# Another order of VectorE's and GpSimd's work in a pair of the cross attention

## The chip, the cores and the metric

The kernel runs on one core of a Trainium2 chip. Its metric is the device time of one execution in microseconds (us). Before the change the median of three runs is 623.79 us, and the runs lie between 623.78 and 624.98 us.

## The reference

One decoder layer on x of shape 4 x 1024 x 256 (32 tiles of 128 rows), with a context of 4 x 77 x 256, all in float32:

```python
x = _layernorm(x + attn(x))            # single head, layer-normed q and k, sigmoid(scores/16 - log S), layerscale
x = _layernorm(x + xattn(ctx, ctx, x)) # 16 heads of 16, softmax over 77 keys, dense
x = _layernorm(x + ffn(x))             # token shift, sigmoid gate, relu squared
```

The change touches the middle line: `logits = q k' / 4` per head, `softmax(logits)`, the product with the values, `dense`, the sum with x, and the second layer norm.

## The kernel before, in words

Every engine has its own instruction queue, written out by hand, and works through it in order; semaphores join the queues. There are three stages. The first is the self attention with the first norm. The second is the cross attention, and the third the feed-forward part. The change is in the second stage alone.

The second stage is a loop over s, one pair of tiles (2s and 2s+1, 256 rows) each, for s = 0 to 15, with three more rounds (16 to 18) that drain it and in which the third stage begins. It is pipelined by hand: in round s the queues hold the logits, maxima and exponentials of pair s, the transposition of the softmax weights of tiles 2s-3 and 2s-2, the product with the values of pair s-2, the dense product and residual of pair s-3, and the second norm of pairs s-3 and s-4. In the same round the query of pair s+2 is made from the normed x.

For one tile t the chain is as follows. TensorE makes the logits (`cross_scores`, L1230) in two halves. VectorE takes the maxima of each half (`maxima`, L846). ScalarE makes the exponentials (`exponentials`, L389). GpSimd adds the halves of a row (`fold_weights`, L607), VectorE sums them (`sums`, L852) and inverts (`reciprocals`, L859), and GpSimd multiplies (`normalise`, L612). TensorE turns the weights in three blocks (`weights_t`, L1246); VectorE copies the first two out (`weights_body`, L866), and ScalarE the third (`weights_tail`, L319). The three blocks of all tiles share two PSUM banks in turn, so a block can be turned only when the block two before it has been copied out. The products with the values (`mixed`, L1263) go to ScalarE and VectorE as a high and a low part (`mixed_hi`, `mixed_lo`, L728), and then to `dense`.

The query of pair s+2 needs a transposition (`x1`), its high part on ScalarE (`x1_hi`) and its low part on VectorE (`x1_lo`, L728); TensorE's `query` is the last item of its round.

The second norm of a pair: VectorE adds the residual (`crossed`, L879) and makes the statistics (`stats2`, L884 and L889). GpSimd makes the deviation and the bias (`deviation2`, L621 to L626). ScalarE norms the first tile (`norm2`, L319) and VectorE the second (`norm2`, a tensor_scalar from SBUF to SBUF, L894). `norm1` (L808) is an instruction of the same kind and shape on VectorE; four of them stand in round 2.

VectorE's queue in a round, in order: `maxima(2s,0)`, `weights_body(2s-3,0)`, `crossed(s-3)`, `maxima(2s,1)`, `weights_body(2s-3,1)`, `sums` and `reciprocals(2s-1)`, `x1_lo(s+2)`, `maxima(2s+1,0)`, `stats2(s-3)`, `weights_body(2s-2,0)`, `mixed_lo(s-2)`, `maxima(2s+1,1)`, `weights_body(2s-2,1)`, `sums` and `reciprocals(2s)`, `norm2(s-4)`.

GpSimd's queue in a round: `fold_weights(2s-1)`, `residual2(s)` (L599), `normalise(2s-1)`, `deviation2(s-3)`, `fold_weights(2s)`, `normalise(2s)`.

ScalarE's queue in a round: `exponentials(2s,0)`, `weights_tail(2s-3)`, `exponentials(2s,1)`, `x1_hi(s+2)`, `norm2(s-4)`, `exponentials(2s+1,0)`, `mixed_hi(s-2)`, `exponentials(2s+1,1)`, `weights_tail(2s-2)`, `query(s+2)`.

TensorE's queue in a round: `cross_scores(2s,0)`, `dense(s-3)`, `weights_t(2s-3,0)`, `cross_scores(2s,1)`, `weights_t(2s-3,1)` and `(2s-3,2)`, `x1(s+2)`, `cross_scores(2s+1,0)`, `weights_t(2s-2,0)`, `mixed(s-2)`, `cross_scores(2s+1,1)`, `weights_t(2s-2,1)` and `(2s-2,2)`, `query(s+2)`.

Of the kernel before, what the change touches and what calls it, by code (L numbers as in the profile page):

```python
# [22 lines left out]
NJ = NT // 2  # L23
# [48 lines left out]
def decoder_layer(nc, io):  # L72
    ctx = ExitStack()
    with ctx:
# [162 lines left out]
        def weights(t):  # L237
            return p_sb[:, t % NP].rearrange("p (h k) -> p h k", k=SP)
# [13 lines left out]
        with nc.Block() as block:  # L252
# [271 lines left out]
            def _(pool):  # L524
# [39 lines left out]
                def deviation1(g):  # L564
                    w.wait_ge(*ln1s_dve.at(g))
                    if g:
                        w.wait_ge(*ln1b_dve.at(g - 1))
                    pool.tensor_tensor(rsl[:], mvl[:, :, 1], eps4, ALU.add).then_inc(ln1s_pool.sem, 1)
                    w.wait_ge(*ln1s_pool.at(g, 1))
                    pool.tensor_tensor(rsl[:], rsl[:], half4, ALU.pow).then_inc(ln1s_pool.sem, 1)  # L570
# [25 lines left out]
                def residual2(i):  # L596
                    w.wait_ge(*tx_pe.at(i))
                    x2 = xs[:, 2 * i:2 * i + 2, :]
                    pool.tensor_tensor(x2, x2, each_tile(bxd[:], 2), ALU.add).then_inc(xr_pool.sem, 1)  # L599

                def fold_weights(t):
                    w.wait_ge(*ex_act.at(4 * t + 3))
                    w.wait_ge(*pads_pool.at(0))
                    if t:
                        w.wait_ge(*sum_dve.at(t - 1))
                    p = weights(t)
                    pool.tensor_tensor(fold[:].rearrange("p (h k) -> p h k", k=FO), p[:, :, 0:FO],  # L607
                                       p[:, :, FO:2 * FO], ALU.add).then_inc(fo_pool.sem, 1)

                def normalise(t):  # L610
                    w.wait_ge(*rc_dve.at(t))
                    pool.tensor_tensor(weights(t), weights(t), rc[:, t % 2].rearrange("p (h o) -> p h o", o=1)  # L612
                                       .to_broadcast([P, H, SP]), ALU.mult).then_inc(pn_pool.sem, 1)

                def deviation2(i):
                    w.wait_ge(*xds_dve.at(i))
                    if i >= 2:
                        w.wait_ge(*ln2_act.at(i - 2))
                        w.wait_ge(*ln2_dve.at(i - 2))
                    r, nb = rs2[:, i % 2], nb2[:, i % 2]  # L620
                    pool.tensor_tensor(r, mv2[:, i % 2, :, 1], eps4[:, 0:2], ALU.add).then_inc(xds_pool.sem, 1)  # L621
                    pool.tensor_tensor(nb, mv2[:, i % 2, :, 0], minus4[:, 0:2], ALU.mult).then_inc(xds_pool.sem, 1)
                    w.wait_ge(*xds_pool.at(i, 1))
                    pool.tensor_tensor(r, r, half4[:, 0:2], ALU.pow).then_inc(xds_pool.sem, 1)
                    w.wait_ge(*xds_pool.at(i, 3))
                    pool.tensor_tensor(nb, nb, r, ALU.mult).then_inc(xds_pool.sem, 1)  # L626
# [64 lines left out]
                for s in range(NJ + 3):  # L691
                    if 1 <= s <= NJ:
                        fold_weights(2 * s - 1)
                        if s < NJ:
                            residual2(s)
                        normalise(2 * s - 1)
                    if s == 1:
                        deviation1(NG - 1)
                    if 0 <= s - 3 < NJ:
                        deviation2(s - 3)  # L700
                    if s < NJ:
                        fold_weights(2 * s)
                        normalise(2 * s)
                    if s == 0:
                        tail_rows()
                    for i in (2 * (s - NJ) - 1, 2 * (s - NJ)):
                        if i >= 0:
                            halo(i)
                            if i >= 3:
                                residual3(i - 3)  # L710
                            if i >= 4:
                                deviation3(i - 4)
                                norm3(i - 4)
# [10 lines left out]
            def _(dve):  # L724
                w = Once(dve)

                def low_part(hi, lo, whole):
                    return dve.tensor_tensor(lo, whole, f(hi), ALU.subtract)  # L728
# [65 lines left out]
                def stats1(g):  # L794
                    for t in range(4):
                        w.wait_ge(*ln1a_dve.at(g, t // 2 + 1))
                        dve.bn_stats(stl[:, t], xs[:, 4 * g + t]).then_inc(ln1s_dve.sem, 1)
                    if g:
                        w.wait_ge(*ln1s_pool.at(g - 1))
                    for t in range(4):  # L800
                        w.wait_ge(*ln1s_dve.at(g, 1 + t))
                        dve.bn_aggr(mvl[:, t], stl[:, t]).then_inc(ln1s_dve.sem, 1)
# [34 lines left out]
                def x1_lo(i):  # L837
                    w.wait_ge(*tx_act.at(i))
                    low_part(*hi_lo(x1T, i % 2), x_bank).then_inc(tx_dve.sem, 1)
# [15 lines left out]
                def reciprocals(t):  # L855
                    w.wait_ge(*sum_dve.at(t))
                    if t >= 2:
                        w.wait_ge(*pn_pool.at(t - 2))
                    dve.reciprocal(rc[:, t % 2], sm[:, t % 2]).then_inc(rc_dve.sem, 1)  # L859
# [9 lines left out]
                def mixed_lo(i):  # L869
                    w.wait_ge(*pv_act.at(i))  # L870
                    if i >= 2:
                        w.wait_ge(*xd_pe.at(i - 2))
                    low_part(*hi_lo(oT, i % 2), pv_bank).then_inc(pv_dve.sem, 1)
# [7 lines left out]
                def stats2(i):  # L881
                    w.wait_ge(*xda_dve.at(i))
                    for t in range(2):
                        dve.bn_stats(st2[:, i % 2, t], xs[:, 2 * i + t]).then_inc(xds_dve.sem, 1)  # L884
                    if i >= 2:
                        w.wait_ge(*xds_pool.at(i - 2))
                    for t in range(2):
                        w.wait_ge(*xds_dve.at(i, 1 + t))
                        dve.bn_aggr(mv2[:, i % 2, t], st2[:, i % 2, t]).then_inc(xds_dve.sem, 1)  # L889
# [134 lines left out]
                for s in range(NJ + 3):  # L1024
                    if 0 < s < NJ:
                        maxima(2 * s, 0)
                    if 0 <= 2 * s - 3 < NT:
                        weights_body(2 * s - 3, 0)
                    if 0 <= s - 3 < NJ:
                        crossed(s - 3)  # L1030
                    if 0 < s < NJ:
                        maxima(2 * s, 1)
                    if 0 <= 2 * s - 3 < NT:
                        weights_body(2 * s - 3, 1)
                    if 1 <= s <= NJ:
                        sums(2 * s - 1)
                        reciprocals(2 * s - 1)
                    if s + 2 < NJ:
                        x1_lo(s + 2)
                    if s < NJ:  # L1040
                        maxima(2 * s + 1, 0)
                    if s == 2:
                        norm1(NG - 1)
                    if 0 <= s - 3 < NJ:
                        stats2(s - 3)
                    if 0 <= 2 * s - 2 < NT:
                        weights_body(2 * s - 2, 0)
                    if 0 <= s - 2 < NJ:
                        mixed_lo(s - 2)
                    if s < NJ:  # L1050
                        maxima(2 * s + 1, 1)
                    if s == 0:
                        stats1(NG - 1)
                    if 0 <= 2 * s - 2 < NT:
                        weights_body(2 * s - 2, 1)
                    if s < NJ:
                        sums(2 * s)
                        reciprocals(2 * s)
                    if 0 <= s - 4 < NJ:
                        norm2(s - 4)  # L1060
                    for i in (2 * (s - NJ) - 1, 2 * (s - NJ)):
                        if i >= 0:
                            if i >= 1:
                                mix_lo(i - 1)
                            if i >= 3:
                                stats3(i - 3)
                            mixes(i)
                            if i >= 2:
                                gated(i - 2)
                            if i >= 1:  # L1070
                                key_squares_lo(i - 1)
# [387 lines left out]
```

## Time and profile before

| what | value |
|---|---|
| median of three runs | 623.79 us |
| the profiled execution's own time | 621.29 us |
| its span (first to last instruction) | 619.2 us |
| mean granted TensorE clock | 0.982 |
| PE, DVE, ACT, POOL busy over the span | 551.2, 453.1, 366.4, 344.9 us |
| chain that ended last: PE, DVE, ACT, POOL | 58%, 15%, 12%, 6% |

The second stage runs from about 301 us to about 506 us of the span. PE is TensorE, DVE is VectorE, ACT is ScalarE and POOL is GpSimd. A busy time is the time in which an engine worked on instructions, and successive instructions of DVE and ACT overlap by some 0.08 to 0.13 us in the trace, so the cost of one in a queue is the distance between two starts. The chain is followed back from the last instruction of the program to what released each step.

### The profile page before, as it was taken

Reading aid. Unit: us, or ns where it says so; the run is one execution under the profiler, and the core shown is the slowest. Engines: PE = TensorE matmul, PEld = TensorE weight load, DVE = VectorE, ACT = ScalarE, POOL = GpSimd, SP = SyncE. Lnnn points to the kernel's source line nnn. Section 1 sums busy time; section 2 is a strip of 40 time slices with the busy share of each in tenths; the row PEclk is TensorE's granted clock in tenths of the full one; section 3 lists DMA queues with packets and bytes.
Section 4 is the critical chain, followed back from the end, with each engine's and each line's share of the span. In section 5 each row is a group of like instructions: output and inputs, shape, how many; then the busy total and the mean of one; then the engine's idle time right before and its main releaser. Section 6 shows DMA issues by size and latency. Waiting matters only on the chain.

```text
span 619.2 us, 11109 instructions
## 1 busy us (share of the span) xinstructions
PE 551.2 (89%) x3952; PEld 455.2 (74%) x3952; DVE 453.1 (73%) x1050; ACT 366.4 (59%) x984; POOL 344.9 (56%) x377
## 2 busy tenths in 40 slices
PE   3879999999999999999868998999899968798884
PEld 2769989898989899888645665666566557788883
DVE  3976566777766676765467788888888976898885
ACT  1245444344444444433676788788878847788882
POOL 3545253433525351415177687788778960588885
PEclk9999999999999999999987999999999998999998
DMA  5221001010130002100000000000000000011112
GB/s 174 68 69 48 23 0 52 19 52 18 51 104 1 1 25 77 52 2 0 2 0 2 1 1 2 2 2 1 2 2 1 2 2 1 17 36 52 52 48 72
DMA packets 18351, 17.53 MB, mean 28 GB/s; under 512 B 1836, under 2 KB 18297, under 8 KB 18297
## 3 DMA queue, kind: packets, MB, share of 16 engines
q1 hardware_dynamic: 18024, 16.57, 8.4%
q8 instruction: 31, 0.51, 0.3%
q10 hardware_dynamic: 272, 0.26, 0.1%
q14 instruction: 24, 0.19, 0.1%
HBM read 12.63 MB, written 4.19 MB: 27 GB/s over the span
## 4 chain that ended last, share of the span: by engine, by line
PE 58%; DVE 15%; ACT 12%; POOL 6%; issue 5%; DMA 1%; SPq 1%; POOLq 0%; DVEq 0%; ACTq 0%
PE ring L215 29%; PE big L215 17%; PE ring L1246 4%; ACT p_sb L389 4%; PE big L1230 3%; POOL p_sb L612 2%; PE ring L1139 2%; DVE neg_mx L846 2%; POOL fold L607 2%; DVE pT L866 2%; DVE kkT_lo L728 1%; DVE st L884 1%; ACT kr L440 1%; ACT kkT_hi L450 1%; ACT pT L319 1%
## 5 line engine op out<-in xcount | busy, mean ns | idle before, releaser
L389 ACT ACTIVATE p_sb<-big,neg_mx 128x77 f32<-128x77 f32 x384 | 89.8, 344 | 34.9 <-DVE neg_mx L846 34.9
L728 DVE TENSOR_TENSOR aT_lo<-a_sb,aT_hi 128x512 fp32r<-128x512 f32 x64 | 45.6, 712 | 79.0 <-ACT aT_hi L319 79.0
L612 POOL TENSOR_TENSOR p_sb<-p_sb,rc 128x1248 f32<-128x1248 f32 x32 | 73.1, 2283 | 31.8 <-DVE rc L859 31.8
L1246 PE MATMUL ring<-ident,p_sb 128*128 128x128 f32 (+1 forms) x384 | 58.7, 283 | 21.8 <-DVE pT L866 20.4
L215 PE MATMUL big<-vv_hi,aT_hi 128*128 128x256 f32 x256 | 72.7, 284 | 3.4 <-DVE xs L792 3.4
L352 ACT ACTIVATE a_sb<-ring,nlogs 128x512 f32<-128x512 f32 x64 | 43.5, 680 | 53.6 <-PE ring L215 53.5
L1246 PEld LDWEIGHTS ring<-ident,p_sb 128*128 128x128 f32 (+1 forms) x384 | 39.6, 130 | 46.0 <-DVE pT L866 23.6
L215 PE MATMUL big<-vv_hi,aT_lo 128*128 128x256 f32 x256 | 72.4, 283 | 0.0
L215 PE MATMUL big<-vv_lo,aT_hi 128*128 128x256 f32 x256 | 72.4, 283 | 0.0
L1230 PE MATMUL big<-kb,xq 64*128 64x308 f32 x192 | 51.5, 481 | 4.7 <-ACT p_sb L389 4.0
L215 PEld LDWEIGHTS big<-vv_hi,aT_hi 128*128 128x128 f32 x256 | 48.8, 191 | 8.1 <-issue 5.8
L215 PE MATMUL ring<-qkT_hi 128*128 128x512 f32 x128 | 51.7, 404 | 0.0
L607 POOL TENSOR_TENSOR fold<-p_sb 128x624 f32<-128x624 f32 x32 | 48.8, 1524 | 4.7 <-ACT p_sb L389 4.7
L215 PEld LDWEIGHTS big<-vv_lo,aT_hi 128*128 128x128 f32 x256 | 48.8, 191 | 2.2
L215 PE MATMUL ring<-qkT_lo,qkT_hi 128*128 128x512 f32 x128 | 50.2, 392 | 0.0
L215 PE MATMUL ring<-qkT_hi,qkT_lo 128*128 128x512 f32 x128 | 49.9, 390 | 0.0
L546 POOL TENSOR_TENSOR rs<-mv,consts 128x2 f32<-128x2 f32 x32 | 12.5, 391 | 65.9 <-DVE mv L760 65.9
L215 PEld LDWEIGHTS big<-vv_hi,aT_lo 128*128 128x128 f32 x256 | 48.8, 191 | 0.0
L866 DVE COPY pT<-ring 128x512 f32<-128x512 f32 x64 | 43.6, 681 | 5.0 <-PE ring L1246 5.0
L846 DVE TENSOR_REDUCE neg_mx<-big 128x4 f32<-128x308 f32 x96 | 42.2, 468 | 2.3 <-PE ring L1230 2.1
L556 POOL TENSOR_TENSOR vv_lo<-v_sb,vv_hi 128x512 fp32r<-128x512 f32 x16 | 21.1, 1316 | 40.5 <-ACT vv_hi L319 40.5
L319 ACT ACTIVATE xT_hi<-xraw 128x512 fp32r<-128x512 f32 x16 | 10.1, 631 | 55.7 <-PE big L215 50.0
(160 smaller groups left out, 1757.1 us busy)
## 6 DMA issues: line engine op xcount, KB each, us to landing
xraw<-in_xT SPq DMA_DIRECT2D x16, 256.0 KB, 2.6
xs<-in_x SPq DMA_DIRECT2D x8, 512.0 KB, 3.9
out_y<-y SPq DMA_DIRECT2D x16, 256.0 KB, 2.1
cT<-in_cT SPq DMA_DIRECT2D x1, 308.0 KB
wraw<-in_wqT ACTq DMA_DIRECT2D x1, 256.0 KB, 3.9
wraw<-in_wkT SPq DMA_DIRECT2D x1, 256.0 KB, 4.3
wv_raw<-in_wv SPq DMA_DIRECT2D x1, 256.0 KB, 5.8
wo_ls<-in_woT SPq DMA_DIRECT2D x1, 256.0 KB, 5.7
```

What stands on the lines that cost most here:

```text
L215: mm = pe.matmul(out, s_, m_, start=first and k == 0 and q == 0, stop=last and k == n - 1 and q == 2, skip_group_check=not check)
L319: return act.activation(out, in_, ACT.Identity, **kw)
L352: act.activation(a_sb[:, i % NAR], st_bank[i % 2], ACT.Sigmoid, bias=nlogs[:, 0:1], scale=1.0 / 16).then_inc(st_act.sem, 1)
L389: ex = act.activation(weights(t)[:, HG * g + h, 0:SC], logits[g][:, h * SC:(h + 1) * SC], ACT.Exp, bias=neg_mx[:, t % 2, HG * g + h:HG * g ...
L556: pool.tensor_tensor(lo, tiles(v_sb[:, i % 2]), f(hi), ALU.subtract).then_inc(v_pool.sem, 1)
L607: pool.tensor_tensor(fold[:].rearrange("p (h k) -> p h k", k=FO), p[:, :, 0:FO], p[:, :, FO:2 * FO], ALU.add).then_inc(fo_pool.sem, 1)
L612: pool.tensor_tensor(weights(t), weights(t), rc[:, t % 2].rearrange("p (h o) -> p h o", o=1) .to_broadcast([P, H, SP]), ALU.mult).then_inc ...
L728: return dve.tensor_tensor(lo, whole, f(hi), ALU.subtract)
L846: dve.tensor_reduce(neg_mx[:, t % 2, HG * g:HG * (g + 1)], logits[g][:, 0:LW].rearrange("p (h k) -> p h k", k=SC), AX, ALU.min)\
L866: dve.tensor_copy(pT[:, t // 2 % 2, c, :, (t % 2) * P:(t % 2 + 1) * P], tiles(tp_bank[(3 * t + c) % 2], NH)).then_inc(tp_dve.sem, 1)
L1230: mm = pe.matmul(logits[2 * e + r][:, 0:LW], xq[half, i % 2, e * D + u * P:e * D + (u + 1) * P], kb[half, b, e], start=True, stop=True)
L1246: mm = pe.transpose(tp_bank[n % 2][0:rows, g * P:(g + 1) * P], p_sb[:, t % NP, c0:c0 + rows], ident[:])
```

## The change

VectorE's queue in a round gets another order in its second half, and `deviation2` on GpSimd goes behind `normalise(2s)`. No instruction is added or removed.

```diff
@@ GpSimd
                         deviation1(NG - 1)
-                    if 0 <= s - 3 < NJ:
-                        deviation2(s - 3)
                     if s < NJ:
                         fold_weights(2 * s)
                         normalise(2 * s)
+                    if 0 <= s - 3 < NJ:
+                        deviation2(s - 3)
@@ VectorE
                         sums(2 * s - 1)
                         reciprocals(2 * s - 1)
-                    if s + 2 < NJ:
-                        x1_lo(s + 2)
                     if s < NJ:
                         maxima(2 * s + 1, 0)
                     if s == 2:
                         norm1(NG - 1)
-                    if 0 <= s - 3 < NJ:
-                        stats2(s - 3)
                     if 0 <= 2 * s - 2 < NT:
                         weights_body(2 * s - 2, 0)
-                    if 0 <= s - 2 < NJ:
-                        mixed_lo(s - 2)
+                    if s + 2 < NJ:
+                        x1_lo(s + 2)
                     if s < NJ:
                         maxima(2 * s + 1, 1)
                     if s == 0:
                         stats1(NG - 1)
+                    if 0 <= s - 2 < NJ:
+                        mixed_lo(s - 2)
                     if 0 <= 2 * s - 2 < NT:
                         weights_body(2 * s - 2, 1)
                     if s < NJ:
                         sums(2 * s)
                         reciprocals(2 * s)
+                    if 0 <= s - 3 < NJ:
+                        stats2(s - 3)
                     if 0 <= s - 4 < NJ:
                         norm2(s - 4)
```

## Rows read from the trace of the kernel before

**Rows 1.** Busy time by engine over one round (stretch, length, then busy, count).
```profile
389.10:401.46 12.36, 11.45 (x102) 7.97 (x102) 10.62 (x25) 10.28 (x41) 9.95 (x10) 1.00 0.01 2
```

**Rows 2.** Chain that ended last: one step in two rounds (start, length).
```profile
399.40 0.62 PE ring L1246 x4
...
411.76 0.62 PE ring L1246 x4
```

**Rows 3.** Timeline of DVE in one round (start, length, idle before and releaser).
```profile
390.50 0.32 DVE L894 TENSOR_SCALAR xs<-xs,mv,rs 128x256 f32<-128x256 f32 x1
...
394.47 0.80 DVE L852 TENSOR_REDUCE sm<-fold 128x16 f32<-128x624 f32 x1
395.31 0.25 DVE L859 RECIPROCAL rc<-sm 128x16 f32<-128x16 f32 x1
396.42 0.69 DVE L728 TENSOR_TENSOR x1T_lo<-ring,x1T_hi 128x512 fp32r<-128x512 f32 x1 [0.85 <-ACT x1T_hi L319]
397.02 0.47 DVE L846 TENSOR_REDUCE neg_mx<-big 128x4 f32<-128x308 f32 x1
...
397.80 0.74 DVE L884 BATCH_NORM_STATS2 st<-xs 128x6 f32<-128x256 f32 x2
...
398.67 0.67 DVE L866 COPY pT<-ring 128x512 f32<-128x512 f32 x1
399.89 0.69 DVE L728 TENSOR_TENSOR oT_lo<-ring,oT_hi 128x512 fp32r<-128x512 f32 x1 [0.54 <-ACT oT_hi L319]
```

**Rows 4.** Timeline of ACT in the same round.
```profile
393.62 0.59 ACT L319 ACTIVATE pT<-ring 56x512 f32<-56x512 f32 x1 [0.29 <-PE ring L1246]
394.11 1.79 ACT L389 ACTIVATE p_sb<-big,neg_mx 128x77 f32<-128x77 f32 x8
395.78 0.61 ACT L319 ACTIVATE x1T_hi<-ring 128x512 fp32r<-128x512 f32 x1
396.25 0.62 ACT L319 ACTIVATE xs<-xs,nb,rs 128x256 f32<-128x256 f32 x1
...
399.20 0.65 ACT L319 ACTIVATE oT_hi<-ring 128x512 fp32r<-128x512 f32 x1
```

**Rows 5.** All instructions of L808 (count, then shortest, median, longest in ns).
```profile
L808 DVE TENSOR_SCALAR xs<-xs,mvl,rsl x32: 398/408/1595, 93.8 to 334.0; 128x256 f32<-128x256 f32 x32
```

**Rows 6.** Timelines of DVE and POOL in round 2.
```profile
331.25 0.97 DVE L808 TENSOR_SCALAR xs<-xs,mvl,rsl 128x256 f32<-128x256 f32 x1
...
329.80 2.28 POOL L612 TENSOR_TENSOR p_sb<-p_sb,rc 128x1248 f32<-128x1248 f32 x1
332.03 1.56 POOL L607 TENSOR_TENSOR fold<-p_sb 128x624 f32<-128x624 f32 x1
```

**Rows 7.** Timelines of DVE and PE in round 14.
```profile
480.41 0.68 DVE L866 COPY pT<-ring 128x512 f32<-128x512 f32 x1
...
483.67 0.79 PE L1230 MATMUL big<-kb,xq 64*128 64x308 f32 x4
```

**Rows 8.** Timeline of POOL, normalise of tiles 26, 30 and 31.
```profile
477.21 2.29 POOL L612 TENSOR_TENSOR p_sb<-p_sb,rc 128x1248 f32<-128x1248 f32 x1 [1.41 <-DVE rc L859]
...
499.56 2.29 POOL L612 TENSOR_TENSOR p_sb<-p_sb,rc 128x1248 f32<-128x1248 f32 x1 [1.20 <-DVE rc L859]
...
504.53 2.28 POOL L612 TENSOR_TENSOR p_sb<-p_sb,rc 128x1248 f32<-128x1248 f32 x1 [1.20 <-DVE rc L859]
```

**Rows 9.** Timeline of DVE in rounds 16 and 17.
```profile
504.37 0.69 DVE L884 BATCH_NORM_STATS2 st<-xs 128x6 f32<-128x256 f32 x2
...
505.19 0.67 DVE L866 COPY pT<-ring 128x512 f32<-128x512 f32 x1
...
515.03 0.69 DVE L728 TENSOR_TENSOR oT_lo<-ring,oT_hi 128x512 fp32r<-128x512 f32 x1 [1.96 <-ACT oT_hi L319]
```

**Rows 10.** Timeline of POOL, first instructions of deviation2 and the fold behind it.
```profile
484.42 0.20 POOL L621 TENSOR_TENSOR rs<-mv,consts 128x2 f32<-128x2 f32 x1
...
485.65 1.52 POOL L607 TENSOR_TENSOR fold<-p_sb 128x624 f32<-128x624 f32 x1
```

## The prediction

> **What bounds the kernel now.** I read the busy time by engine over one round first. In the middle of the second stage TensorE works 11.45 us of a round and no other engine over 10.62 us [rows 1]. The chain that ended last repeats itself every 411.76 - 399.40 = 12.36 us [rows 2], so a round costs 0.91 us more than TensorE's work. The chain passes through tail copy and exponentials on ScalarE, x1_hi, then on VectorE x1_lo, maxima(2s+1,0), stats2 and the copy of a turned block, and only then back to TensorE. In VectorE's timeline the reader sees why: after the reciprocal (ends 395.56) it sits idle 0.85 us for x1_lo, then come maxima and statistics, and the copy that frees TensorE's bank ends only at 399.34 [rows 3]; the transposition of the third block starts at 399.40 [rows 2]. It idles 0.54 us more for mixed_lo [rows 3].
>
> **What the change takes away.** After the reciprocal stand now maxima(2s+1,0), whose logits are ready, and the copy. The copy ends 0.77 + 0.68 = 1.45 us after the start of the maxima, about 397.0 and not 399.34. TensorE's 0.91 us go, and the next bound would be TensorE's own 11.45 us, if nothing else grows. GpSimd loses nothing by its edit at first sight: deviation2 (1.23 us, from 484.42 to the fold at 485.65 [rows 10]) goes behind normalise(2s), and fold(2s) comes earlier.
>
> **What it adds.** No instruction is new, so the question is what each now stands beside. The pair's end is reciprocals(2s), stats2, norm2. GpSimd starts normalise(2s) 0.08 us after the reciprocal ends (at 504.53, the reciprocal ends 504.45, which is 0.08 us behind the start of the statistics [rows 8, 9]) and works on it 2.28 us. Statistics do not mind: beside exactly such a normalise they took 505.19 - 504.37 = 0.82 us, against 398.67 - 397.80 = 0.87 us with GpSimd idle [rows 3, 8, 9]. But norm2 is a tensor_scalar from SBUF to SBUF. Before, it started at 390.50, directly behind the reciprocal and ahead of normalise, and took 0.32 us [rows 3]. Its sister L808 shows what happens behind the start of a GpSimd instruction: median 408 ns, but 966 ns for the one issued at 331.25 while normalise ran (329.80 to 332.08); it ended at 332.22, 0.14 us after GpSimd's instruction. The one behind it met the fold (332.03 to 333.59) and is the longest of all, 1595 ns [rows 5, 6]. So such an instruction waits until the running GpSimd instruction is over, and ends 0.14 us later. The Trainium skill, page "SBUF — State Buffer", section on SBUF's two separate sides, gives the reason: VectorE in a two-port mode and GpSimd share one port pair, which whoever starts first holds for its whole instruction. By that rule, the trace agrees. This rule speaks against the change.
>
> In the new order norm2 is issued 0.74 us after the reciprocal's end (0.82 - 0.08), while normalise runs until 0.08 + 2.28 = 2.36. It ends at 2.50, not at 1.06: a stall of 1.44 us per round, from round 4, the first with a norm2.
>
> **The round, walked with the stall.** Zero is the end of reciprocals(2s-2). Costs in a queue are distances between starts (length less 0.08 us of overlap): maxima of one half pair 0.77, copy 0.60, each of x1_lo, mixed_lo and crossed 0.60 (all 512 wide with one operand in PSUM), sums 0.84, reciprocal 0.25 [rows 3].
> VectorE: maxima(2s,0) at 2.42, copy 3.19, crossed 3.79, maxima(2s,1) 4.39, copy (2s-3,1) 5.16, sums 5.76, reciprocal 6.60 to 6.85, maxima(2s+1,0) 6.77, copy 7.54, x1_lo 8.14, free at 8.74. GpSimd is in time: normalise 2.36, deviation2 3.59, fold(2s-1) 5.1, against sums at 5.76.
> TensorE: the copy at 5.16 frees block (2s-2,0). In round 14 it was 483.67 + 0.79 - 480.41 = 4.05 us from that copy's start to the end of the logits (2s+1,1) [rows 7]; so maxima(2s+1,1) starts at 5.16 + 4.07 = 9.23, VectorE is free again at 10.00.
> ScalarE: its first exponentials start 0.51 us behind the maxima (0.47 for the first bank, 0.04 to react), at 2.93; a half tile is 395.78 - 394.11 = 1.67 us. Then tail copy 0.49, exponentials 1.67, x1_hi 0.47, its own norm2 0.49 (0.62 less the overlap), exponentials 1.67: mixed_hi starts at 9.39 and mixed_lo 0.69 us later (399.89 - 399.20), at 10.08 [rows 3, 4]. The tail copy does not wait longer: TensorE turns its block 0.62 us behind the copy of 3.19 (ends 3.87), ready about 4.55; ScalarE comes at 4.60.
> VectorE again: copy 10.68, sums 11.28, reciprocal 12.12 to 12.37. **The new round takes about 12.37 us**, against 12.36 us. The loop that closes is ScalarE's row of work plus VectorE's end of the pair; TensorE, with 0.9 us idle again, is not it.
>
> **The ends of the stage.** All in time against before; minus is earlier.
> - Rounds 0 to 3: no norm2, so no stall; there TensorE's 0.9 us are gained once (round 3), and some tenths in rounds 0 to 2, which hang on GpSimd and on norm1 (pinned by GpSimd's two instructions of rows 6). I take -1.1 at reciprocals(25).
> - Within a round the second normalise now comes sooner after the first: 12.37 - 6.85 = 5.5 us. Before it was 7.4: mixed_lo at 399.89, then 0.60 + 0.77 + 0.60 + 0.84 + 0.25 to 402.95, from 395.56 [rows 3]. That is a shift of -1.9, so normalise(26), at 477.21 before, comes at -3.0.
> - Rounds 14 and 15 have no x1 and no query. Before, GpSimd bound them: 499.56 - 477.21 = 22.35 us for two [rows 8]. Now the stall stays: maxima(2s+1,1) ends at 10.00, mixed_lo follows at once, 12.3 us a round, 24.6 for two. +2.25, sum -0.75.
> - normalise(30) to normalise(31) was 4.97 us [rows 8]; deviation2 now stands between, +1.23, sum +0.5.
> - Round 16: the statistics no longer stand ahead of the copy of 505.19 [rows 9], -0.82, sum -0.3.
> - Round 17: the statistics stood in the idle 1.96 us ahead of mixed_lo (515.03) [rows 9]; now they stand behind it and ahead of the third stage's low parts, +0.87, sum +0.6.
> With nine rounds at +0.01 the sum is +0.6 to +0.7 us. The profiled execution, 621.29 us of which 619.2 are its span, would become 621.9. It lies 2.5 us under the median of 623.79; I add the difference to the median: **624.4 us**.
>
> The unknown costs, from both sides. Of a round: 0.1 us less, if ScalarE's exponentials react faster (its maxima and starts lie 0.47 to 0.51 us apart), or 0.15 us more, if the tail copy waits (its margin is 0.05 us); eleven rounds make -1.1 and +1.7. Of the moved mixed_lo and x1_lo: nothing to 0.1 us, since both have later readers. Rounds 0 to 3: -2 to 0; TensorE's clock there is part of that, because in round 2 it idles some 3 us in both orders. Main case: 622.4 to 626.8.
>
> **The rivals.**
> - *The stall does not come* (norm2 isn't held, or the statistics push it to where it is harmless). For it: the median of L808's 32 is 408 ns. Against: those had no long GpSimd instruction beside them; here normalise always starts first. Then VectorE's round is 12.37 - 1.44 = 10.9, GpSimd's loop, by rounds 14 and 15 that it bound, 22.35 / 2 = 11.2 [rows 8], and TensorE's 11.45 binds: -0.91 for nine rounds, -8.2, with -3.0 at normalise(26) as above, nothing in rounds 14 and 15, +1.2 for deviation2 behind them, and -0.82 and +0.87 at the end: about -10, 613.8 us.
> - *Half of it*: ScalarE or TensorE arrives so that only 0.5 us of the stall counts in the loop. A round of 11.9 us, -0.45 for nine rounds, -4.1, with the ends as in the main case: 620.3 us.
> - *Slower: the stall makes ScalarE's tail copy late.* The place is round s's first tail copy: TensorE turns its block only behind VectorE's copy of 3.19, which the stall moves. From the point at which that block is ready later than 4.60, each tenth is a tenth per round. With 0.3 us (TensorE still busy with dense when the copy is done) it is 12.7 a round and eleven times 0.3: +3.3, 627.7 us. For it: a margin of 0.05 us. Against: TensorE has 0.9 us to spare.
> - *Nothing moves*: as before within 0.3 us, 623.8. It can't be told from the main case.
>
> **How the numbers follow.** A measurement of this kernel can tell about 0.2% from no change, 1.25 us: faster is below 622.5, slower above 625.0. Main case with its twin 0.62, of which 0.04 below 622.5 and 0.19 above 625.0; no stall 0.11; half 0.10; tail copy late 0.17. Faster 0.25, same 0.39, slower 0.36. The range for 8 in 10 is 619.5 to 628.2; it leaves out the case without a stall. The main case's own is 622.4 to 626.8.
>
> **What would show it.** Right: L894 with a mean near 1.76 us instead of 0.32, each ending about 0.14 us behind a normalise; the round at 12.3 to 12.5 us; TensorE's waits for the third block's bank gone from (2s-2,2) but its work still near 11.45 of the round, with waits spread over (2s-3,2) and (2s-2,0); rounds 14 and 15 near 12.3 us and not 11.2; normalise(2s) directly behind its reciprocal with deviation2 behind it without a wait. Wrong: L894 still at 0.32 us, a round of 11.4 to 11.6 us, TensorE without idle time in the middle of the stage; or a tail copy that waits over 0.3 us for TensorE.

## The result: 0.67% slower, and the profile after

The changed kernel takes 627.92 us, the median of 18 runs between 625.16 and 630.78, against 623.75 us for the kernel before (18 runs, 620.89 to 625.33). The ratio is 1.0067 with a 95% interval of 1.0047 to 1.0087: 4.2 us slower in the medians. The profiled execution took 626.28 us with a span of 624.5 us, 5.3 us more than the span before. A second profile of the same kernel (below, `r_after_again`) has a span of 624.3 us and the same pattern. Where span times are compared below, they are single profiled executions.

The busy time over one round of the changed kernel, between two starts of normalise(2s) (as in [rows 1]: behind the length, the busy time and number of instructions of TensorE, of its weight loads, of VectorE, ScalarE and GpSimd):

```profile
398.98:411.34 12.36, 11.50 (x101) 7.97 (x102) 11.79 (x25) 10.01 (x41) 9.96 (x9) 1.00 0.01 2
```

The round is 12.36 us long, as before [rows 1, 2]. VectorE is now busy 11.79 us of it and not 10.62. Its own timeline shows with what, and GpSimd's beside it shows why:

```profile
399.64 1.77 DVE L894 TENSOR_SCALAR xs<-xs,mv,rs 128x256 f32<-128x256 f32 x1
```
```profile
398.98 2.28 POOL L612 TENSOR_TENSOR p_sb<-p_sb,rc 128x1248 f32<-128x1248 f32 x1 [1.76 <-DVE rc L859]
401.22 0.24 POOL L621 TENSOR_TENSOR rs<-mv,consts 128x2 f32<-128x2 f32 x1
```

normalise(2s) ends at 398.98 + 2.28 = 401.26, and norm2 at 399.64 + 1.77 = 401.41, 0.15 us later. Before, it took 0.32 us [rows 3]. It is so in all twelve rounds with both, 4 to 15; the other four, in the drain, meet no long GpSimd instruction and take 0.38 to 0.40 us. The row of all sixteen (shortest, median, longest in ns):

```profile
L894 DVE TENSOR_SCALAR xs<-xs,mv,rs x16: 381/1767/1769, 362.6 to 546.7; 128x256 f32<-128x256 f32 x16
```

The chain that ended last, from the stall through the rest of that round (start, length; x2 is two instructions). The reader sees that it runs along VectorE and crosses to TensorE only for block (2s-2,0), the product with the values and one half of the logits:

```profile
399.64 1.38 DVE xs L894
401.33 0.85 DVE neg_mx L846 x2
402.18 0.60 DVE pT L866
402.78 0.60 DVE xs L879
403.38 0.77 DVE neg_mx L846 x2
404.15 0.61 DVE pT L866
404.89 0.63 PE ring L1246 x4
405.52 1.86 PE ring L1263 x32
407.38 0.74 PE big L1230 x4
408.15 0.86 DVE neg_mx L846 x2
409.01 0.64 DVE oT_lo L728
```

Where the rounds end up in time is read from normalise of tiles 26, 28, 30 and 31 in GpSimd's timeline, to be laid beside [rows 8]:

```profile
473.11 2.28 POOL L612 TENSOR_TENSOR p_sb<-p_sb,rc 128x1248 f32<-128x1248 f32 x1 [1.76 <-DVE rc L859]
...
485.41 2.28 POOL L612 TENSOR_TENSOR p_sb<-p_sb,rc 128x1248 f32<-128x1248 f32 x1 [1.72 <-DVE rc L859]
...
497.71 2.28 POOL L612 TENSOR_TENSOR p_sb<-p_sb,rc 128x1248 f32<-128x1248 f32 x1 [1.72 <-DVE rc L859]
503.94 2.27 POOL L612 TENSOR_TENSOR p_sb<-p_sb,rc 128x1248 f32<-128x1248 f32 x1 [1.20 <-DVE rc L859]
```

Up to normalise(31) the changed kernel is not slower at all, but 504.53 - 503.94 = 0.6 us ahead. All of the loss comes behind it. Rounds 16 and 17, the drain, lose 5.5 us, and the rest of the third stage 0.4 us: -0.6 + 5.5 + 0.4 = 5.3 us of span. In the drain VectorE's timeline runs:

```profile
506.90 0.69 DVE L728 TENSOR_TENSOR oT_lo<-ring,oT_hi 128x512 fp32r<-128x512 f32 x1 [2.50 <-ACT oT_hi L319]
...
510.65 1.67 DVE L916 SCALAR_TENSOR_TENSOR big<-ring,mu,carry 128x256 f32<-128x256 f32 x4 [1.28 <-POOL carry L633]
...
519.07 0.69 DVE L728 TENSOR_TENSOR oT_lo<-ring,oT_hi 128x512 fp32r<-128x512 f32 x1 [4.97 <-ACT oT_hi L319]
519.68 0.74 DVE L884 BATCH_NORM_STATS2 st<-xs 128x6 f32<-128x256 f32 x2
...
520.56 0.38 DVE L894 TENSOR_SCALAR xs<-xs,mv,rs 128x256 f32<-128x256 f32 x1
520.85 1.28 DVE L728 TENSOR_TENSOR xmT_lo<-big,xmT_hi 128x512 fp32r<-128x512 f32 x2
```

The same two instructions of the third stage, its first mixes (L916) and its first low part (L728 of xmT), in the kernel before:

```profile
508.75 1.67 DVE L916 SCALAR_TENSOR_TENSOR big<-ring,mu,carry 128x256 f32<-128x256 f32 x4 [1.35 <-ACT carry L319]
...
515.96 1.28 DVE L728 TENSOR_TENSOR xmT_lo<-big,xmT_hi 128x512 fp32r<-128x512 f32 x2
```

The third stage's first low part starts 520.85 - 503.94 = 16.9 us behind normalise(31). Before it was 515.96 - 504.53 = 11.4 us, so 5.5 us are lost here. This distance is called the drain's length below. TensorE's timeline in the drain says what is slow:

```profile
500.79 0.62 PE L1246 MATMUL ring<-ident,p_sb 128*56 128x128 f32 x4 [2.15 <-DVE pT L866]
...
503.02 3.17 PE L1263 MATMUL ring<-pT,vb 128*32 128x256 f32 x32
...
512.96 1.06 PE L1246 MATMUL ring<-ident,p_sb 128*56 128x128 f32 x4 [2.76 <-DVE pT L866]
514.75 3.64 PE L1263 MATMUL ring<-pT,vb 128*32 128x256 f32 x32 [0.73 <-DVE pT L866]
```

The products with the values of pairs 14 and 15 take 3.17 and 3.64 us; before, both took 1.93:

```profile
502.49 1.93 PE L1263 MATMUL ring<-pT,vb 128*32 128x256 f32 x32
...
512.41 1.93 PE L1263 MATMUL ring<-pT,vb 128*32 128x256 f32 x32 [0.73 <-ACT pT L319]
```

TensorE had idled 2.15 us for the copy behind norm2(11), which stalls at the end of round 15, and 2.76 us in round 17; in the kernel before these two waits were 0.28 and 1.80 us. In the rows by stretch the third number from the end is the granted clock, a mean between 1.00 (2.4 GHz) and 0.50 (1.2 GHz). TensorE was at the lower level for a part of each stretch below; before, it was 1.00 all the way from 500 to 516 us:

```profile
500.00:504.00 4.00, 2.54 (x20) 1.51 (x24) 3.13 (x7) 1.08 (x2) 2.72 (x6) 0.77 0.00 0
504.00:508.00 4.00, 4.00 (x43) 2.43 (x36) 1.50 (x3) 1.34 (x3) 2.22 (x1) 0.80 0.01 4
...
512.00:516.00 4.00, 2.31 (x17) 1.19 (x21) 2.10 (x4) 1.84 (x4) 0.00 (x0) 0.55 0.00 0
516.00:520.00 4.00, 3.40 (x28) 1.61 (x20) 0.93 (x2) 1.16 (x3) 0.00 (x0) 0.59 0.00 0
```

### The profile page after: what moved, and what is told of

It reads as the page before. It is cut to its first block, busy times and chain, and to the rows that moved or that the text cites. A ratio compares the mean times of both kernels' runs of the same rounds, so it can differ in the third digit from the quotient of the medians.

```text
span 624.5 us, 11109 instructions
## 1 busy us (share of the span) xinstructions
PE 553.6 (89%) x3952; PEld 454.9 (73%) x3952; DVE 468.2 (75%) x1050; ACT 363.2 (58%) x984; POOL 345.1 (55%) x377
## 4 chain that ended last, share of the span: by engine, by line
PE 55%; DVE 26%; ACT 7%; issue 6%; POOL 4%; DMA 1%; SPq 1%; POOLq 0%; DVEq 0%; ACTq 0%
PE ring L215 24%; PE big L215 17%; PE ring L1263 5%; DVE neg_mx L846 4%; DVE pT L866 3%; DVE xs L894 3%; PE ring L1246 2%; PE big L1230 2%; PE ring L1139 2%; DVE sm L852 2%; DVE st L884 1%; DVE kkT_lo L728 1%; DVE oT_lo L728 1%; DVE xs L879 1%; ACT kr L440 1%
## 5 line engine op out<-in xcount | busy, mean ns | idle before, releaser
L728 DVE TENSOR_TENSOR aT_lo<-a_sb,aT_hi 128x512 fp32r<-128x512 f32 x64 | 45.6, 712 | 78.9 <-ACT aT_hi L319 78.9
L1230 PE MATMUL big<-kb,xq 64*128 64x308 f32 x192 | 50.1, 471 | 4.7 <-ACT p_sb L389 4.0
```

The costliest lines, as they stand in the source:

```text
L1230: mm = pe.matmul(logits[2 * e + r][:, 0:LW], xq[half, i % 2, e * D + u * P:e * D + (u + 1) * P], kb[half, b, e], start=True, stop=True)
```

## The experiments

Theory A: the stall of norm2 eats what the new order of maxima and copies gains. Theory C: the drain loses time by the place of stats2 in it, and, C2, by TensorE's clock. Theory D: the drain is late through the last stall, that of round 15. The rivals are those of each run's own expectation. Each ratio is to the kernel before in runs on the same chip; that kernel's median differs between chips (620.6 to 623.4 us), so ratios are compared and not times.

### Theory A

**norm2 ahead of the statistics** (`e1_norm2_first`), changed kernel with

```diff
                         reciprocals(2 * s)
-                    if 0 <= s - 3 < NJ:
-                        stats2(s - 3)
                     if 0 <= s - 4 < NJ:
                         norm2(s - 4)
+                    if 0 <= s - 3 < NJ:
+                        stats2(s - 3)
```

> The changed kernel with one swap: norm2 on VectorE stands directly behind the second reciprocals, ahead of stats2, so that it is issued before normalise(2s) starts. Theory A (the stall of 1.44 us a round, VectorE's tensor_scalar held by GpSimd's running instruction, is what eats the gain): L894 falls from 1.77 to 0.32 us, the round from 12.36 to 11.4 to 11.6 us, TensorE has no idle time in the middle of the stage; rounds 14 and 15 take about 11.2 us; the time is 9 to 12 us under the changed kernel's 627.9, near 617. Rival B (the stall is beside the limit, ScalarE's or TensorE's loop holds the round at 12.36 us anyway): L894 short again, the round still 12.2 us or more, the time within 2 us of 627.9.

Measured: 612.08 us, ratio 0.9868 (0.9842 to 0.9894). L894's instructions, and one round, between two starts of a normalise:

```profile
L894 DVE TENSOR_SCALAR xs<-xs,mv,rs x16: 320/322/855, 361.1 to 532.2; 128x256 f32<-128x256 f32 x16
```
```profile
401.31:412.57 11.26, 11.26 (x107) 8.01 (x103) 10.42 (x25) 10.15 (x40) 9.88 (x10) 1.00 0.00 1
```

The swap of two neighbours is worth 2% against the changed kernel (0.9868 against 1.0067). TensorE has no idle time in the round any more; the round is 11.26 us, even below the 11.4 expected. The longest of L894, 855 ns, is norm2(12) in the drain: there it comes behind the start of normalise(31) and ends 492.89 + 0.85 = 493.74, again 0.14 us after it (491.32 + 2.28 = 493.60). The drain is 505.45 - 491.32 = 14.1 us long, so this version still loses 2.7 us there; the product of pair 15 took 3.04 us.

**The stall alone** (`e4_stall_alone`), kernel before with

```diff
                         maxima(2 * s, 0)
+                    if 5 <= s < NJ:
+                        norm2(s - 5)
...
-                    if 0 <= s - 4 < NJ:
+                    if 0 <= s - 4 < NJ and s >= NJ - 1:
                         norm2(s - 4)
```

> The kernel before, with one instruction moved in rounds 5 to 14: norm2 on VectorE goes behind maxima(2s,0) of the next round, so that it is issued 0.8 us after normalise started. Nothing else is changed. Theory A: L894 takes 1.5 to 1.8 us instead of 0.32 in those rounds, VectorE's copy of the first turned block and maxima(2s,1) come 1.1 us later, ScalarE's chain 0.6 to 1.1 us later, the round is 13.0 to 13.4 us and the time 6 to 10 us over the kernel before. Rival (an instruction of this kind isn't held by GpSimd's; L808's long ones have another cause): L894 stays at 0.32 us and the time within 0.5 us of the kernel before.

Measured: 631.75 us, ratio 1.0164 (1.0128 to 1.0200), 11 us slower for one small instruction moved by one place. All of L894, then the same tile's normalise in two successive rounds:

```profile
L894 DVE TENSOR_SCALAR xs<-xs,mv,rs x16: 320/1876/1879, 366.1 to 552.8; 128x256 f32<-128x256 f32 x16
```
```profile
371.57 2.28 POOL L612 TENSOR_TENSOR p_sb<-p_sb,rc 128x1248 f32<-128x1248 f32 x1 [1.04 <-DVE rc L859]
...
384.69 2.28 POOL L612 TENSOR_TENSOR p_sb<-p_sb,rc 128x1248 f32<-128x1248 f32 x1 [1.04 <-DVE rc L859]
```

A round is 13.12 us, 0.76 more than before. In the old order about half of the 1.55 us of stall reaches the loop. The 11 us are more than the 6 to 10 expected. In the profile TensorE's clock fell as well: the products of pairs 13 and 15 took 3.00 and 3.39 us instead of 1.93, so not all of the 11 us is the stall.

**The second tile's norm on ScalarE** (`e11_norm2_on_scalar`), changed kernel with ScalarE's norm2 doing both tiles and VectorE's taken out

```diff
+                    copy(xs[:, 2 * i + 1], xs[:, 2 * i + 1], bias=nb2[:, i % 2, 1:2], scale=rs2[:, i % 2, 1:2])\
+                        .then_inc(ln2_dve.sem, 1)
...
-                    if 0 <= s - 4 < NJ:
-                        norm2(s - 4)
...
-                norm2(NJ - 1)
```

> The changed kernel with the second tile's norm2 moved from VectorE to ScalarE; VectorE keeps its new order otherwise, stats2 at the pair's end. Theory A (port shared by VectorE's tensor_scalar and GpSimd's instruction): no instruction is held any more, since ScalarE's of the same shape took 0.62 us beside GpSimd's work; ScalarE's row of work grows by 0.5 us a round; VectorE's shrinks by 1.7; a round of 11.3 to 11.6 us and 8 to 10 us under the changed kernel in its rounds. Rival B (whatever norms the second tile waits there, for the deviation or for xs, not for the port): ScalarE shows an instruction of over 1 us or an idle time ahead of it, and the round stays at 12 us or more.

Measured: 614.26 us, ratio 0.9889 (0.9863 to 0.9916). ScalarE's two norms take 1.11 us together, with no wait ahead and none inside; normalise of tile 2s comes every 408.98 - 397.55 = 11.43 us:

```profile
403.31 1.11 ACT L319 ACTIVATE xs<-xs,nb,rs 128x256 f32<-128x256 f32 x2
```
```profile
397.55 2.28 POOL L614 TENSOR_TENSOR p_sb<-p_sb,rc 128x1248 f32<-128x1248 f32 x1 [1.32 <-DVE rc L861]
...
403.73 2.27 POOL L614 TENSOR_TENSOR p_sb<-p_sb,rc 128x1248 f32<-128x1248 f32 x1
...
408.98 2.28 POOL L614 TENSOR_TENSOR p_sb<-p_sb,rc 128x1248 f32<-128x1248 f32 x1 [1.48 <-DVE rc L861]
```

ScalarE norms the same rows with the same deviations, partly beside a normalise (403.73 to 406.00), and nothing is held or waits for data. Rival B, that the norm waits for its data, falls.

This run also says something of the drain. It has the changed order of stats2 there and no stall, and TensorE's clock stayed at 1.00 from 480 to 504 us, also behind a wait of 2.49 us. Its timelines of GpSimd, TensorE and VectorE:

```profile
494.21 2.28 POOL L614 TENSOR_TENSOR p_sb<-p_sb,rc 128x1248 f32<-128x1248 f32 x1 [1.20 <-DVE rc L861]
...
500.56 0.62 PE L1245 MATMUL ring<-ident,p_sb 128*56 128x128 f32 x4 [2.49 <-DVE pT L868]
501.91 1.93 PE L1262 MATMUL ring<-pT,vb 128*32 128x256 f32 x32 [0.73 <-ACT pT L319]
...
506.01 1.25 DVE L730 TENSOR_TENSOR xmT_lo<-big,xmT_hi 128x512 fp32r<-128x512 f32 x2
```

The drain is 506.01 - 494.21 = 11.8 us long, against 11.4 before and 16.9 in the changed kernel.

**Maxima and copy alone** (`e5_maxima_copy_only`), kernel before with

```diff
-                    if s + 2 < NJ:
-                        x1_lo(s + 2)
                     if s < NJ:
                         maxima(2 * s + 1, 0)
                     ...
-                    if 0 <= s - 3 < NJ:
-                        stats2(s - 3)
                     if 0 <= 2 * s - 2 < NT:
                         weights_body(2 * s - 2, 0)
+                    if s + 2 < NJ:
+                        x1_lo(s + 2)
+                    if 0 <= s - 3 < NJ:
+                        stats2(s - 3)
```

> The kernel before with one part of the change alone: maxima(2s+1,0) and the copy of the turned block stand ahead of x1_lo and stats2; norm2, mixed_lo and GpSimd's order as before. Theory A: no stall (L894 at 0.32 us), TensorE's 0.91 us of a round are gained at least in part. deviation2 stands ahead of fold(2s) and waits for the statistics, about as long as before, so GpSimd's loop decides: a round of 11.5 to 12.0 us and 4 to 9 us under the kernel before. Rival (the gain needs all of the new order, mixed_lo behind the maxima above all, since ScalarE's loop holds the round): 12.2 us or more a round, within 2 us of the kernel before.

Measured: 613.12 us, ratio 0.9852 (0.9816 to 0.9888), 10.3 us under the kernel before (623.38 on its chip), more than the 4 to 9 expected. One round:

```profile
398.37:410.08 11.71, 11.43 (x103) 7.97 (x101) 10.53 (x25) 10.12 (x40) 9.92 (x9) 1.00 0.01 2
```

These moves alone bring all but about half a per cent of the most that any version here reached (0.9804).

### Theory C: the drain

**Statistics at the old place in the drain** (`e3_old_drain`), changed kernel with

```diff
+                    if NJ <= s and s - 3 < NJ:
+                        stats2(s - 3)
                     if 0 <= 2 * s - 2 < NT:
                         weights_body(2 * s - 2, 0)
...
-                    if 0 <= s - 3 < NJ:
+                    if 3 <= s < NJ:
                         stats2(s - 3)
```

> The changed kernel, but in rounds 16 to 18 stats2 is at its old place; rounds 0 to 15 as changed, the stall with them. Theory C (statistics' place in the drain costs some 2 us ahead of the first mixes and 0.9 us ahead of the third stage's low parts): 2 to 4 us under the changed kernel, 624 to 626, the first mixes about 5 us behind normalise(31) instead of 6.7. Rival D (the drain is late because norm2 of round 15 holds VectorE 1.4 us, TensorE idles 2.15 us and its clock is granted at half): under 1 us gained, the products with the values of pairs 14 and 15 still at 3.2 and 3.7 us.

Measured: 623.30 us, ratio 1.0028 (1.0011 to 1.0045), so the old order in the drain gives back 0.4 to 0.5% of the kernel's time. From normalise(31) to the first low part it is 516.47 - 505.04 = 11.4 us, as before, with norm2(11) still stalled (1.76 us). TensorE's two products are at full speed, though the first comes behind the same wait of 2.15 us as in the changed kernel:

```profile
501.89 0.62 PE L1248 MATMUL ring<-ident,p_sb 128*56 128x128 f32 x4 [2.15 <-DVE pT L866]
...
503.74 1.93 PE L1265 MATMUL ring<-pT,vb 128*32 128x256 f32 x32
...
512.92 1.93 PE L1265 MATMUL ring<-pT,vb 128*32 128x256 f32 x32 [0.73 <-ACT pT L319]
```

The clock fell in this profile too, only earlier, in round 15, in which nothing differs from the changed kernel. The row of that stretch has a granted clock of 0.72; the product of pair 13 took 3.08 us, and normalise(30) came 498.82 - 491.75 = 7.1 us behind normalise(29) instead of 5.5:

```profile
490.00:496.00 6.00, 5.62 (x48) 2.77 (x45) 3.26 (x8) 4.50 (x19) 4.91 (x3) 0.72 0.00 0
```

So the gain is measured, but this run can't tell how much of it is the order and how much a clock that fell at a cheaper place.

**The last stall taken out** (`e6_last_stall_out`), changed kernel with norm2 ahead of stats2 for `s >= NJ - 1` only.

```diff
+                    if s >= NJ - 1 and 0 <= s - 4 < NJ:
+                        norm2(s - 4)
                     if 0 <= s - 3 < NJ:
                         stats2(s - 3)
-                    if 0 <= s - 4 < NJ:
+                    if 0 <= s - 4 < NJ and s < NJ - 1:
                         norm2(s - 4)
```

> The changed kernel, but from round 15 on norm2 on VectorE stands ahead of stats2, so that the stall of round 15 (which delays the copy that TensorE waits 2.15 us for) is gone and the ten before it stay. Theory D (the drain is late through that stall): TensorE's idle time there falls to about 0.8 us, its clock stays at full speed behind it, and the time falls 2 to 4 us below the changed kernel. Rival C (order of the statistics alone): only the 1.4 us of the stall or less, since in the drain GpSimd's chain of folds and multiplications has slack for it.

Measured: 626.67 us, ratio 1.0060 (1.0037 to 1.0082), against 1.0081 (1.0056 to 1.0105) for the changed kernel on the same chip. The intervals overlap: inconclusive. In its profile TensorE's idle time ahead of the third block is 0.74 us and the product of pair 14 takes 1.93 us, as theory D has it, but that of pair 15 takes 3.26 us, and the clock had also fallen in round 15 (the product of pair 13 took 2.35 us). The drain is 522.11 - 507.91 = 14.2 us long.

**Filler for TensorE** (`e7_filler`), changed kernel with 14 transpositions of the identity, read by nobody, in each round from 16 on

```diff
                         weights_t(2 * s - 3, 1)
+                        if s >= NJ:
+                            filler(14)
                         weights_t(2 * s - 3, 2)
```

> The changed kernel with work added that computes nothing: 14 transpositions of the identity into a bank nobody reads, ahead of the third turned block in each of rounds 16 to 18, where TensorE waits 2.15 and 2.76 us. Theory C2 (the drain costs its 5.9 us mostly because TensorE's granted clock falls to half behind those idle times): the products with the values of pairs 14 and 15 take 1.9 us again instead of 3.2 and 3.7, and the time falls 2 to 3 us below the changed kernel though it does more. Rival: the clock isn't what costs; the same time or up to 1 us more.

Measured: 625.07 us (12 runs, 622.42 to 628.62), ratio 1.0029 (1.0005 to 1.0053). TensorE's two products:

```profile
503.05 1.93 PE L1268 MATMUL ring<-pT,vb 128*32 128x256 f32 x32
...
513.08 3.58 PE L1268 MATMUL ring<-pT,vb 128*32 128x256 f32 x32 [0.73 <-ACT pT L319]
```

More work, less time: the first product is at full speed again, the second isn't. The interval ends just below that of the changed kernel on the same chip (1.0056 to 1.0105); the medians lie 3.3 us apart, against 2 to 3 us expected. So the clock is a real part of the loss, and filler ahead of the wait does not hold it everywhere.

**The changed kernel once more** (`r_after_again`).

> The changed kernel again, unaltered, for a comparison on the same chip as the next ones: 4 us over the kernel before (ratio 1.0067), runs spread over several us. If the drain's loss is TensorE's clock (theory C2), the profile shows in each such execution a stretch at half clock between about 500 and 525 us, at a place that may differ from that of the first profile.

Measured: 628.41 us, ratio 1.0081 (1.0056 to 1.0105). In its profile the two products take 3.54 and 3.64 us.

### Versions that beat both

**norm2 ahead, and the old drain** (`e2_norm2_first_old_drain`): the edits of `e1_norm2_first` and `e3_old_drain` together.

> As the one with norm2 ahead of stats2, and in rounds 16 to 18 (in which the stage drains) VectorE's stats2 is at its old place ahead of the copies and mixed_lo. Theory A with theory C (the changed order costs up to 5 us in the drain, through the statistics on the way to the third stage and TensorE's lower clock behind its longer idle times): round 11.4 to 11.6 us and the drain, from normalise(31) to the first product of the third stage, back near 12.2 us from 17.7; 10 us under the kernel before, about 613 to 615. Rival D (the drain's cost came with the stall of norm2 in round 15, not with the order of the statistics): the same time as the kernel with norm2 ahead alone, within 1 us.

Measured: 610.93 us, ratio 0.9841 (0.9823 to 0.9858). The difference from 0.9868 isn't resolved. The expectation counts the drain up to the first product of the third stage, 516.70 - 504.53 = 12.2 us before; here that is 505.49 - 491.77 = 13.7 us. Up to the first low part it is 504.75 - 491.77 = 13.0 us, against 11.4. The product of pair 15 took 3.47 us, behind a wait of 1.80 us, as long as the one in the kernel before, behind which it took 1.93.

**The same with filler** (`e8_best_filler`).

> The kernel with norm2 ahead and the old drain, plus the 14 transpositions of the identity in each of rounds 16 to 18. Theory C2 (TensorE's clock at half for two stretches near 500 and 507 us is what still costs in the drain): the product with the values of pair 15 at 1.9 us instead of 3.5 and 1 to 2 us gained over its twin without filler, ratio about 0.981. Rival: the clock falls elsewhere instead, no gain (0.984).

Measured: 610.36 us, ratio 0.9818 (0.9791 to 0.9844); the drain 504.15 - 492.73 = 11.4 us, and both products took 1.93 us. The gain over its twin is within the intervals.

**norm2 ahead, and stats2 behind the first copy in the drain** (`e9_norm2_first_drain2`).

```diff
                         x1_lo(s + 2)
+                    if NJ <= s and s - 3 < NJ:
+                        stats2(s - 3)
...
-                    if 0 <= s - 3 < NJ:
-                        stats2(s - 3)
                     if 0 <= s - 4 < NJ:
                         norm2(s - 4)
+                    if 3 <= s < NJ:
+                        stats2(s - 3)
```

> The best of both: the changed order in rounds 0 to 15 with norm2 on VectorE ahead of stats2, and in rounds 16 to 18 stats2 directly behind the first copy and ahead of mixed_lo (where the kernel with maxima and copy alone has it, with the shortest drain seen, 11.0 us from normalise(31) to the third stage's first low part). Theory: rounds of 11.27 us as with norm2 ahead, drain 11 to 13 us: 1 to 2 us below the kernel with the old drain's 0.984 of the kernel before, a ratio of 0.982. Rival: the drain depends on where TensorE's clock falls and not on this place; ratio 0.984 to 0.987.

Measured: 609.20 us, ratio 0.9804 (0.9779 to 0.9830), the lowest ratio of all, 12.7 us under the kernel before on its chip (621.92); from 0.9818 and 0.9841 it isn't resolved. Its drain takes 501.92 - 490.90 = 11.0 us and both products 1.93 us:

```profile
488.19 1.93 PE L1265 MATMUL ring<-pT,vb 128*32 128x256 f32 x32
...
498.37 1.93 PE L1265 MATMUL ring<-pT,vb 128*32 128x256 f32 x32 [0.73 <-ACT pT L319]
```

## Why the prediction was right where it was, and where it was not

The forecast was 624.4 us in a range of 619.5 to 628.2; the time is 627.92, inside it but near its upper end. The likeliest class was no change; it is a slowdown, for which the chance was 0.36. That the range holds is in part luck. The main case's own range ends at 626.8, below the measured time; what reached up to 628.2 was the room for a late tail copy, which did not happen. And two errors went opposite ways: the kernel gained about 1.1 us more ahead of the loop than forecast, and lost 5.5 us in the drain, which was forecast to cost nothing. The mechanism of the full rounds was right, and the extra loss lies where the prediction had none.

- **The stall**, 1.44 us by [rows 5, 6]: right. L894 was forecast at 1.76 us and takes 1.77. `e4_stall_alone` and `e11_norm2_on_scalar` show it by itself, in opposite directions. The Trainium skill, "SBUF — State Buffer", section "SBUF: two separate sides", says that whichever of the two engines starts first gets the shared port pair for the whole instruction and that the other fully blocks; all of these runs agree, with ends 0.14 to 0.15 us behind GpSimd's.
- **The round**, 12.37 us: measured 12.36. The loop that closes was misnamed. ScalarE's row was said to close it, at 10.08 us, with VectorE and TensorE 0.08 us short of that. In the chain it is VectorE and TensorE's piece that hold it: maxima(2s+1,1) waited 0.50 us for the logits. Two loops of nearly one length, 10.08 and 10.00 us to the same point, stood in the working, and the prediction picked the wrong one without harm to the number.
- **Rounds 14 and 15**, 12.3 us each: measured 485.41 - 473.11 = 12.30 and 497.71 - 485.41 = 12.30.
- **deviation2 between the last two normalise**, +1.23: measured 6.23 us for 4.97, +1.26.
- **Rounds 0 to 3**, -1.1: too small. normalise(26) came 477.21 - 473.11 = 4.1 us earlier, forecast was 3.0. TensorE's clock may be a part of it: in the stretches 333 to 336, 336 to 339 and 339 to 342 us the granted clock was 0.66, 0.50 and 0.70 before, and 0.82, 0.61 and 1.00 after. The rounds up to 13 are the same program in `r_after_again` and `e3_old_drain`, and normalise(25), 2.2 us early here, is 2.0 and 2.7 us early there; forecast was 1.1. No experiment was made on that, so the cause stays open.
- **Rounds 16 and 17**, forecast -0.82 and +0.87, together nothing: this step failed. Measured is +5.5 us. The two terms priced the statistics by their own length, and three things were missing. First, stats2(13) now stands behind mixed_lo(14) and a copy, and GpSimd's deviation2(13), ahead of the carry's first column in its queue, waits for it. So the first mixes hang on mixed_lo(14), which waited 2.50 us, and start 510.65 - 503.94 = 6.7 us behind normalise(31) and not 508.75 - 504.53 = 4.2. By itself this costs little: without a stall and at full clock they start 4.0 us behind it (`e11_norm2_on_scalar`, 498.24 - 494.21). Second, the stall of round 15 now makes mixed_lo(14) late, where in the old order it cost the drain nothing (11.4 us with the stall, `e3_old_drain`). Third, TensorE's two products ran partly at half clock, 1.2 and 1.7 us more. With the old order there, 11.4 us return (`e3_old_drain`).
- **The slower rival**, a late tail copy: it did not happen; rounds did not grow. Its 627.7 us lies near the measured time by accident.
- **The rival without a stall**, 613.8 us: that is about what `e1_norm2_first` made, 0.9868 of the kernel before or, of 623.79, 615.6 us. TensorE's work in such a round was put at 11.45 us and is 11.26.

How the 5.5 us divide is not settled; single profiles allow an estimate. `e11_norm2_on_scalar` has the changed order without a stall and at full clock and takes 11.8 us, or about 12.1 with the 0.3 us of norm2(13), which VectorE has ahead of the low part in the other versions. `e7_filler` has the order with the stall and the first product at full speed and takes 519.13 - 504.36 = 14.8 us; its slow second product is 3.58 - 1.93 = 1.65 us of that, which leaves 13.1 us. So the order alone is some 0.7 us over 11.4, the last stall through that order about 1.0 us more, and the clock, up to 16.9, about 3.8 us.

What decides where the clock falls stays open. In the changed kernel it fell behind waits of 2.15 and 2.76 us, and in both profiles alike. But it held behind the same 2.15 us in `e3_old_drain` and behind 2.49 us in `e11_norm2_on_scalar`, and it fell behind 1.80 us in `e2_norm2_first_old_drain`, where the kernel before kept it behind an equal wait.

## What to carry to other kernels

When an instruction is moved on VectorE, ask what GpSimd is running at the new place: a tensor_scalar from SBUF to SBUF issued before GpSimd's next long instruction costs 0.3 us, and issued behind its start it costs that instruction's rest. Statistics and reductions, and copies and tensor_tensor operations with an operand in PSUM, were not held at such places here. And price the rounds that drain a pipeline by themselves: few instructions cover a wait there, a stall that the old order hid may show in the new one, and TensorE's granted clock there has to be read in each version anew: two profiles of one kernel had it fall at the same places, and small changes of the order moved it.

## What the runs showed of the hardware

- A VectorE tensor_scalar of 128x256 f32 from SBUF to SBUF ended 0.14 to 0.15 us after the GpSimd instruction that was running when it was issued. GpSimd's instruction lost nothing (2.28 us in all kernels); its next one, 0.20 us long before, took 0.24.
- Batch-norm statistics from SBUF were not held by the same GpSimd instruction, which started 0.16 us behind the first of them: 0.69 us for two in the changed kernel's full rounds, against 0.74 us in the kernel before [rows 3]. Nor were others, by the changed kernel's timeline: 0.68 us for a copy and for x1_lo beside the normalise that started at 393.46 us, and 0.79 us for the sums beside GpSimd's residual2, as with GpSimd idle.
- TensorE's granted clock fell to its lower level in the changed kernel's drain, behind waits of 2.15 and 2.76 us, and the same 32 products took 3.17 to 3.64 us instead of 1.93. A wait's length alone did not decide it: 2.15 and 2.49 us left the clock at 1.00 in other versions, and 1.80 us did not in one. The runs of the changed kernel spread over 5.6 us, and in its results the four with the lowest mean clock (0.969 to 0.971) are the slowest (629.98 to 630.78 us), and those under 626 us have 0.979 to 0.987; but 629.02 us has 0.979 too, so the mean clock does not give the time by itself.
